# Three row groups of a depthwise convolution on ScalarE and GpSimd, and a new order at the end of each image pair

## The reference

```
g = groupnorm(x)                                   # 32 groups: two channels share mean and variance
t2 = conv(g, w2, 1x3)
t3 = einsum('nakhw,nbhw->nakb', g shifted by 2k-6, g) / 56  # 7 correlations of channels, 64x64
x1 = x + conv5x5(g, w8, depthwise, dilation 2)
       - (correlation weights (t3*p6w*p9w) applied to t2 shifted by 7 rows - conv1x5(t2, w7, depthwise))
t  = tokens of x1 (3136 per image)
a  = layernorm(t); q, k = elu(a Wq)+1, elu(a Wk)+1 (16 heads of 64); v = a Wv
t  = t + linear attention with cosine and sine weights of q, k, v, projected by dense_w
b  = layernorm(t); p = softmax over tokens of (b gate_w + gate_b)   # 32 experts
top = the 8 largest p of each expert; pooled = sum of p * b over them
out = t + (per-expert two-layer MLP of pooled) scattered back with weight p
```

## Time and profile before

| | |
|---|---|
| median of three runs | 4075.51 us |
| profiled execution | 4079.0 us |
| its span | 4077.2 us |
| mean granted clock of TensorE | 0.94 of full |
| TensorE matmul busy | 3586.0 us, 88% |
| VectorE busy | 2994.3 us, 73% |
| ScalarE busy | 1687.9 us, 41% |
| GpSimd busy | 1248.6 us, 31% |

### The profile page before, as it was taken

The page is one execution under the profiler, slowest core; times in us unless marked ns, Lnnn a source line. Parts: engine busy times, 40 slices in busy tenths (PEclk is TensorE's granted clock), DMA queues, the critical chain, the costliest instruction groups (busy, mean ns, idle before and its releaser), DMA issues.

```text
span 4077.2 us, 52073 instructions
## 1 busy us (share of the span) xinstructions
PE 3586.0 (88%) x17556; PEld 1798.3 (44%) x17556; DVE 2994.3 (73%) x3523; ACT 1687.9 (41%) x1798; POOL 1248.6 (31%) x1327
## 2 busy tenths in 40 slices
PE   4798998989889998989889899899989898899976
PEld 2344444444544444444444445344444444544453
DVE  6878876788677876788767886778767887548823
ACT  0145533455254534445434553445435554343310
POOL 1015620176013740156201760127501572011100
PEclk8899998999999998999989999999989999899967
DMA  1000000000000001000000000000010000100045
GB/s 47 17 1 1 1 17 25 1 1 1 25 17 1 1 1 41 1 1 1 17 25 1 1 1 25 17 1 1 1 41 1 1 1 16 30 1 1 1 116 200
DMA packets 18676, 70.96 MB, mean 17 GB/s; under 512 B 8781, under 2 KB 13421, under 8 KB 13485
## 3 DMA queue, kind: packets, MB, share of 16 engines
q1 hardware_dynamic: 18365, 67.10, 5.3%
HBM read 37.26 MB, written 29.84 MB: 16 GB/s over the span
## 4 chain that ended last, share of the span: by engine, by line
issue 48%; PE 33%; DVE 8%; POOL 7%; ACT 2%; DMA 1%; SPq 1%; POOLq 0%; DVEq 0%; ACTq 0%
PE ps_D L1499 11%; POOL UA L549 4%; PE ps_E L1463 4%; PE ps_C L1488 3%; PE ps_A L1446 3%; PE ps_B L1446 3%; DVE RR L1106 2%; PE ps_E L1474 1%; DVE region L1076 1%; DVE arena L911 1%; PE ps_C L1417 1%; POOL RS L581 1%; PE ps_E L1512 1%; POOL RR L574 1%; DVE region L1085 1%
## 5 line engine op out<-in xcount | busy, mean ns | idle before, releaser
L562 POOL TENSOR_TENSOR arena<-arena,UHL 128x896 f32<-128x896 f32 x350 | 764.6, 2210 | 226.3 <-ACT UHL L695 211.6
L1499 PE MATMUL ps_D<-region,small 128*128 128x448 f32 x1792 | 785.2, 562 | 32.9 <-DVE OS L1112 32.8
L549 POOL TENSOR_TENSOR UA<-region,CS 128x128 f32<-128x128 f32 (+1 forms) x400 | 178.8, 449 | 1837.8 <-DVE region L986 795.3
L1085 DVE TENSOR_TENSOR region<-region,ps_C 128x896 f32<-128x896 f32 x448 | 485.9, 1085 | 247.9 <-PE ps_C L1488 247.9
L1499 PEld LDWEIGHTS ps_D<-region,small 128*128 128x128 f32 x1792 | 321.2, 194 | 346.7 <-issue 284.8
L734 ACT ACTIVATE EQ<-ps_B,NEG 128x896 f32<-128x896 f32 x224 | 225.6, 1007 | 480.4 <-PE ps_B L1446 480.3
L911 DVE SCALAR_TENSOR_TENSOR arena<-arena,W8C 128x896 f32<-128x896 f32 (+1 forms) x418 | 416.8, 1010 | 1.2
L1417 PE MATMUL ps_C<-region,UA 128*128 128x512 f32 (+1 forms) x800 | 382.7, 601 | 2.9 <-ACT region L627 2.9
L734 ACT ACTIVATE EQ<-ps_A,NEG 128x896 f32<-128x896 f32 x224 | 225.6, 1007 | 350.8 <-PE ps_A L1446 350.7
L695 ACT ACTIVATE UHL<-arena,W8C 128x896 f32<-128x896 f32 x350 | 361.2, 1032 | 0.0
L1052 DVE SCALAR_TENSOR_TENSOR region<-region,ps_B 128x1024 f32<-128x1024 f32 (+1 forms) x200 | 243.9, 1219 | 159.8 <-ACT region L713 156.4
(11 more groups left out here) (310 smaller groups left out, 5772.9 us busy)
## 6 DMA issues: line engine op xcount, KB each, us to landing
arena<-x SPq DMA_DIRECT2D x8, 1568.0 KB, 6.6
t_keep<-Y SPq DMA_DIRECT2D x7, 1568.0 KB, 6.8
w_keep<-region SPq DMA_DIRECT2D x7, 784.0 KB, 5.7
CST<-t_keep SPq DMA_DIRECT2D x2, 1568.0 KB, 10.0
small<-t_keep SPq DMA_DIRECT2D x2, 1568.0 KB, 12.8
plane<-w_keep SPq DMA_DIRECT2D x4, 784.0 KB, 15.9
UHL<-t_keep SPq DMA_DIRECT2D x2, 1568.0 KB, 12.3
out<-CST SPq DMA_DIRECT2D x2, 1568.0 KB, 11.7
```

The source lines that it names most:

```text
L562: pool.tensor_tensor(out=X[:, cut], in0=X[:, cut], in1=PRODUCT[m % 3], op=ALU.add).then_inc(pool_taps.sem, 1)
L1085: dve.tensor_tensor(out=q, in0=q, op=ALU.mult, in1=here.area(key)[:, :].rearrange("p (c n) -> p c n", c=2)[:, :, 0:PIX])\
L1499: ins = pe.matmul(here.area(key)[:, 0:PIX], MW[i][:, c, :], Q[s % 3][:, c, :], start=c == 0, stop=c == NCHUNK - 1)
```

## The change

- GpSimd and ScalarE take three of the four row groups (75 pieces) instead of two (50). The first 30 of them are done beside K tiles 20 to 49, one per tile, the other 45 in Q slots from slot 3. VectorE keeps the narrow group, 25 pieces, one per K tile from tile 19.
- The square roots of ScalarE and the reciprocals of VectorE in the layer and group norms become a power of -0.5 on GpSimd (`deviations`, `group_norm`), in GpSimd's queue behind the UA product of a tile or the sum of a slot. The scaling of the second layer norm comes one slot later.
- `correlations` and its copies (`columns`) go ahead of the tokens' second transposes and the logits. In `back`, TensorE does two convolutions, two token transposes with the third convolution between them, then weights and pooled tokens, the fourth convolution and the split. VectorE does the maximum, the residuals of groups 0 and 1 around the shares, both layer norms, and the residuals of groups 2 and 3 last. The low part of group 1 goes to K tile 0.
- Pooled tokens are computed with the 64 weight columns in alternating halves of the array, copied, and turned with `BOTH` (both halves' identities), which adds up the halves.
- Tile numbers of norms and splits shift, and PSUM areas are named instead of handed round.

The diff, cut to its core:

```diff
--- before
+++ after
-POOL_UNITS = 2
+POOL_UNITS = 3
 POOL_PIECES = 25 * POOL_UNITS
...
-SUM_TILES = [None, None, 0, 4]
...
-SCALE_TILES = [None, None, 9, 10]
-SPLIT_TILES = [None, None, 11, 12]
-UTS_TILES = [None, 2, 13, 15]
+SUM_TILES = [None, None, 1, 5]
+STD_TILES = [None, None, 6, 10]
+SCALE_TILES = [None, None, 8, 12]
...
 FIRST_TAPS = TAPS[:25 - DIAGONALS] + TAPS[25:]
 FIRST_PIECES = len(FIRST_TAPS) * NG
-STATS_TILE, MEAN_TILE, CENTRE_TILE, VAR_TILE, NORM_TILE = 3, 12, 13, 15, 16
+STATS_TILE, MEAN_TILE, CENTRE_TILE, VAR_TILE, SPREAD_TILE, NORM_TILE = 3, 13, 13, 15, 16, 18
 K_PIECES, FRONT_PIECES, Q_PIECES, DRAIN_PIECES = 1, PIECES, (1, 0, 0, 1), 1
-PRODUCT_SLOT, POOL_LAG = 3, 4
+PRODUCT_TILE, PRODUCT_SLOT, POOL_LAG = 20, 3, 4
+TILE_PRODUCTS = KTILES - PRODUCT_TILE
 SLOTS = 4 * STEPS
 DEN_LAG, SUM_LAG, RECIP_LAG, RB_LAG, OUT_LAG, PARTS_LAG, FOLD_LAG = 4, 5, 6, 8, 9, 13, 18
...
-            uses = [(("ucol", g), misc()) for g in range(len(COLGROUPS))]
-            uses += [("t3", "D")]
-            uses += [(("wt", g), misc()) for g in range(2)] if routing else []
-            uses += [("t3t", misc())] + ([("pool", "E")] if routing else [])
-            for g in range(NG):
-                uses += [(("conv", g), misc())]
-                uses += [(("yt", g - 1), misc())] if g in (1, 2) else []
-                uses += [(("uts", i, 0), misc()) for i in range(2)] if g == 2 else []
-            return uses
+            uses = [("t3t", "C"), (("conv", 0), "A"), (("conv", 1), "B"), (("yt", 0), "C"), (("conv", 2), "A"),
+                    (("yt", 1), "B")]
+            uses += [(("wt", 0), "C"), (("wt", 1), "B"), ("pool", "E")] if routing else []
+            uses += [(("conv", 3), "C")] + ([("pool_turned", "E")] if routing else [])
...
+            def deviations(sums, std, pair, g, turn):
+
+                pool.wait_ge(*sums.at(pair, g + 1))
+                passed(pool)
+                pool.tensor_scalar(ST[:, g % 2, 2, :], ST[:, g % 2, 1, :], 1.0 / C, LN_EPS, ALU.mult, ALU.add)\
+                    .then_inc(variance.sem, 1)
+                pool.wait_ge(*turn)
+                pool.tensor_tensor(out=ST[:, g % 2, 3, :], in0=ST[:, g % 2, 2, :], op=ALU.pow,
+                                   in1=NEGH[:, 0:1].broadcast_to([P, 2 * GROUP])).then_inc(std.sem, 1)
+
+            def group_norm(here):
+
+                pool.wait_ge(*here.emptied("gvar"))
+                pool.tensor_tensor(out=MV[:, 7:8], in0=MV[:, 6:7], in1=NEGH[:, 0:1], op=ALU.pow)\
+                    .then_inc(gn_scale.sem, 1)
+
             def pair_of_images(here):
                 pair = here.pair
+
...
+                        deviations(ln1_sums, ln1_std, pair, STD_TILES.index(k), variance.at(pair, STD_TILES.index(k) - 1))
+                    if here.span == "loop" and k == SPREAD_TILE:
+                        group_norm(here)
+                    if here.span == "loop" and k >= PRODUCT_TILE:
+                        tap_sum(k - PRODUCT_TILE)
...
+                for g in range(2) if here.span == "loop" else ():
+                    deviations(ln1_sums, ln1_std, pair + 1, g, variance.at(pair, 3 + NG + g))
+
+            group_norm(Here("setup"))
+            for g in range(2):
+                deviations(ln1_sums, ln1_std, 0, g, variance.first(g + 1))
             with pool.Fori(0, PAIRS - 1) as pair:
                 pair_of_images(Here("loop", pair))
             pair_of_images(Here("last", PAIRS - 1))
-            pool.wait_ge(*Here("last").emptied("pool"))
+            pool.wait_ge(*Here("last").emptied("pool_turned"))
             pool.memset(OD, 0.0).then_inc(od_zeroed.sem, 1)
...
-                        for g in (2, 3):
-                            deviations(ln1_sums, ln1_std, pair, g)
-                    if k in SPLIT_TILES:
+                    if k in SPLIT_TILES[2:]:
                         high_part(pair, SPLIT_TILES.index(k))
                     if k in UTS_TILES:
                         split_tokens(here, UTS_TILES.index(k))
-                    if k == VAR_TILE and here.span == "loop":
-                        group_norm(here)
+                    if here.span == "loop" and k >= PRODUCT_TILE:
+                        tap_product(here, pair + 1, k - PRODUCT_TILE)
                     if k == TILES + 2:
...
+                    if here.span == "loop" and PRODUCT_SLOT <= j < PRODUCT_SLOT + POOL_PIECES - TILE_PRODUCTS:
+                        tap_product(here, pair + 1, TILE_PRODUCTS + j - PRODUCT_SLOT)
                     if j in LN2_SLOTS:
                         tokens(here, 2, LN2_SLOTS[j])
-                    if j - 5 in LN2_SLOTS:
-                        deviations(ln2_sums, ln2_std, pair, LN2_SLOTS[j - 5])
                     if here.span == "loop" and j in FRONT_SLOTS:
...
-            def group_norm_apply(here):
-                dve.wait_ge(*here.emptied("gvar"))
-                link(dve.reciprocal(MV[:, 7:8], MV[:, 6:7]))
+            def group_norm_spread(here):
+                dve.wait_ge(*here.filled("gvar"))
+                dve.tensor_scalar(MV[:, 6:7], here.area("gvar")[:, 0:1], GN_EPS, None, ALU.add)\
+                    .then_inc(*here.empty("gvar"))
+
+            def group_norm_apply(pair):
+                dve.wait_ge(*gn_scale.at(pair, 1))
                 dve.tensor_scalar(g_window(4, 0, H), X.rearrange("p (h w) -> p h w", w=W),
...
@@ -1011,35 +1038,45 @@
                 link(dve.reciprocal(MX[:, 10:11], MX[:, 9:10]))
                 dve.tensor_scalar(EW, EW, MX[:, 10:11], None, ALU.mult).then_inc(w_ready.sem, 1)
+            def pool_sums(here):
+
+                dve.wait_ge(*here.filled("pool"))
+                dve.tensor_copy(OS[:, 1, 0:P], here.area("pool")[:, 0:P]).then_inc(*here.empty("pool"))
+
             def pooled(here):
-                dve.wait_ge(*here.filled("pool"))
+                dve.wait_ge(*here.filled("pool_turned"))
                 for i in range(2):
                     ins = dve.tensor_copy(
                         PT[0:C, :, bass.ds(2 * here.pair + i, 1)].rearrange("p e a -> p (e a)"),
-                        here.area("pool")[i * C:(i + 1) * C, i * EXPERTS:(i + 1) * EXPERTS])
-                ins.then_inc(*here.empty("pool"))
+                        here.area("pool_turned")[0:C, i * EXPERTS:(i + 1) * EXPERTS])
+                ins.then_inc(*here.empty("pool_turned"))
...
+                    depthwise(here, pair, FIRST_PIECES)
+                else:
+                    depthwise(here, pair, PIECES)
+                    taps(here)
+                    dve.wait_ge(*t_stored.at(before, 1))
+                    routing(here)
+                conv_residual(here, pair, 0)
                 if before is not None:
-                    routing(here)
-                    depthwise(here, pair, 7)
                     shares(here)
+                conv_residual(here, pair, 1)
+                norm_sums(here, 1, ln1_sums, 0)
+                norm_sums(here, 1, ln1_sums, 1)
+                norm1_scale(pair, 0)
                 if before is not None:
-                    depthwise(here, pair, PIECES)
-                else:
-                    depthwise(here, pair, 51)
-                taps(here)
-                if before is None:
-                    depthwise(here, pair, PIECES)
+                    pool_sums(here)
+                low_part(pair, 0)
+                norm1_scale(pair, 1)
                 if before is not None:
-                    dve.wait_ge(*t_stored.at(before, 1))
                     pooled(here)
-                for g in range(NG):
-                    conv_residual(here, pair, g)
-                    if g in (1, 2):
-                        norm_sums(here, 1, ln1_sums, g - 1)
-                        norm1_scale(pair, g - 1)
-                        low_part(pair, g - 1)
+                conv_residual(here, pair, 2)
+                conv_residual(here, pair, 3)
             def k_features(here, k):
...
                         group_norm(pair + 1, k - STATS_TILE)
                     if conv and k == CENTRE_TILE:
                         group_norm_variance(here)
+                    if conv and k == SPREAD_TILE:
+                        group_norm_spread(here)
                     if conv and k == NORM_TILE:
-                        group_norm_apply(here)
+                        group_norm_apply(pair + 1)
                     if conv and k > NORM_TILE:
-                        depthwise(here, pair + 1, K_PIECES)
+                        depthwise(here, pair + 1, K_PIECES, DVE_PIECES)
...
@@ -1161,8 +1200,8 @@
                     for part in range(4):
                         if j - 1 - part in LN2_SLOTS:
                             norm_part(here, 2, ln2_sums, LN2_SLOTS[j - 1 - part], part)
-                    if j - 6 in LN2_SLOTS:
-                        norm_scale(2, ln2_std, pair, LN2_SLOTS[j - 6]).then_inc(un2_ready.sem, 1)
+                    if j - 7 in LN2_SLOTS:
```

(47 more changed lines are left out.)

98 lines of the change are left out of this document (54 added, 44 removed).

## The result

The changed kernel takes 3845.6 us (median of 4 runs, 3844.4 to 3850.3) against 4074.7 us: a ratio of 0.944, 95% interval 0.942 to 0.946. A second measurement on another chip gave 0.9427 (0.9414 to 0.9441). The forecast was 3936 us: the sign and the places were right, the gain was 229 us instead of 139.

The account below looks back on a forecast made before the run. Turns of 478.0 us dominate, with a serial end where VectorE becomes the chain. Terms -12 - 5.5 + 8 - 10 = -19.5 us per turn, times 7, and -3 for the last pair give 3936 us; range 3868 to 4015.

Parts of the forecast that it names:

- shared access: K tiles 20 to 43: VectorE and GpSimd exclude each other, 3.0 us a tile; +8 us per turn, bounds 0 and +30.
- Q steps: Q steps without pieces on VectorE get shorter: sum -10 us per turn, bounds -3 and -14.
- early K tiles: Tiles 0 to 19: two waits and the square roots' table loads go; -5.5 us per turn, bounds -2 and -6.
- pooled tokens: End of turn: column halves take 3.5 us instead of 5.93, all under VectorE's chain, so 0.
- End of turn: Reordered end: next K tile starts at 3035.5 instead of 3047.7; gain 12 us, 8 with more waits, 15 with none.
- first layer norm's pair: Q steps: this step pair becomes like the second one, 39.4 to 33.6 us, -5.8.
- steps 3 to 6: Q steps: four steps of 14.6 us on average become 13.5 without VectorE's pieces, -4.3 us.
- Last pair: After the seven turns: the last pair loses some table loads and cold pooling, about -3 us.
- Rival 4: Nothing lost in the K tiles and no waits at the end: -34.5 us per turn, 3831 us; chance 0.05.
- Rivals 1 and 2: K tiles 20 to 43: VectorE and GpSimd lock step, 4090 us, chance 0.07; Q steps gain nothing, 4006 us, 0.14.
- Rival 3: GpSimd's power is dear: at 6 us each all gain goes, at 8 us 4200 us; chance 0.06.
- the cover: Powers on GpSimd, taken as 1 us each, are hidden by other work at every place: 0.

Follow-up runs that it names:

- e3: Changed kernel with VectorE's 25 narrow pieces moved from K tiles 19 to 43 into Q slots, two per step; ratio 0.959 to the kernel before.
- e11: Changed kernel with all tiles of layer norm, split and mean where the kernel before has them, powers still on GpSimd; ratio 0.952 to the kernel before.
- e12: e11 with square roots of one column back on ScalarE as well; ratio 0.954 to the kernel before.
- e7: Changed kernel plus an unused one-column square root on ScalarE at each power, bringing the table loads back; 3854.5 us.
- e4: Changed kernel with 16 of VectorE's narrow pieces in every second K tile and 9 in the first five Q steps; ratio 0.939 to the kernel before.
- e5: Changed kernel with 16 of VectorE's narrow pieces in every second K tile and 9 in Q steps 2 to 6; 3829.7 us.
- e9: e5 with convolution 2's residual ahead of the pooled copy and the second layer norm's scaling; ratio 0.938 to the kernel before.
- e13: e5 with the pooled copy first, then convolution 2's residual, then the second layer norm's scaling; 3817.9 us against 3829.7 for e5.
- e2: Kernel before with only the pieces' part: three row groups on ScalarE and GpSimd, 30 of 75 pieces beside K tiles; ratio 0.982.

## Why the prediction was off

The mechanisms stood in the right places, and the terms of the sum were mis-sized, all to the same side. The steps that failed: the price of the shared access (+8 us for +3.5), the sum of the Q steps (-10 for -15 to -16), in which the first two steps stood at nothing, and, smaller, the early K tiles and the pooled tokens, which stood at 0. Forecast per turn against measured, in the last turn and as the mean of six:

- **End of turn, -12: measured -11.8, mean -13.4.** Chain, waits (1.8 us for 2.0) and the pooled tokens (3.2 us for 3.5) came as worked out, and the first K tile waits for the residual, as forecast, and for the transposes' copy as well. What failed is the 0 for the pooled tokens. In the kernel before they stand in TensorE's chain ahead of the first convolution, and in three of seven turns they take 9.5 us instead of 5.93, with an end longer by 4.8 us; I had read one turn without it. Now they lie under VectorE's chain at 3.2 and at 4.9 us alike (e3). No run has the new order without the halves, so what the halves alone are worth is open.
- **Early K tiles, -5.5 with -6 as the bound: measured -7.6, mean -6.8.** The tiles' shifts make 4.9 us of the mean (e11). I had summed the two stalls and their half clock and taken the rest for token transposes, which stay; TensorE now has 0.4 us of waits there, so three smaller ones went too: 0.7 us with the tiles (it is back in e11), 0.8 and 0.4 us with the square roots (waits like them are back in e12). The roots are worth about 1 us with the old tiles and 0.7 with the new (e12, e7). Ten of them and the loads back cost 1.3 us in a turn.
- **Shared access, +8: measured +3.5, mean +3.4.** The mechanism is shown (e3: gone with the pieces), the price was 2.79 us a tile instead of 3.0. I added two small gaps that are not there, and 0.47 us of hold where the rows have 0.38 (UA's 0.78 less 0.40): 24 x 0.21 = 5.0 us. The other 1.5 us I put down to the buffers, as in the forecast; no run shows it by itself. "0.78 + 2.08" overlap by 0.07. VectorE's piece waits for the end of GpSimd's sum and UA for the end of the piece; the K feature runs beside the sum. The Trainium skill (SBUF — State Buffer, SBUF: two separate sides) calls this an exclusive lock held for the whole instruction; the trace agrees, with a piece of 1.73 us beside a sum and 0.68 alone.
- **Q steps, -10 with -14 as the bound: measured -16.0, mean -14.9.** The steps that I priced came out: the first layer norm's pair 33.6 us as forecast, steps 3 to 6 -2.8 for -4.3. Not priced were the first two steps: 9.3 and 11.9 us instead of 11.4 and 14.0. I take VectorE for the chain there, as the reciprocal, the split and the scaling have no work ahead of them, and e4 bears it out: with pieces back in these steps they take 3.0 us more. I had looked for what the pieces cost only where I had a pair of equal steps with and without them. Before, TensorE then worked at half clock in step 2, after 2.21 us of waiting: 0.58 us for a Q projection's matmul, 0.35 in the changed kernel. Another 3 us came in the second layer norm's pair and behind the last step. e3 shows that the pieces on VectorE do it: with them back in the Q steps, and GpSimd's work as in the changed kernel, Q is 247.1 us.
- **Last pair, -3: measured -8.8.** Pooled tokens take 5.5 us instead of 11.1 in this colder stretch, of which 4.9 are left behind the turning; the final adds give 3.7 and the K tiles 2.5, and the Q steps take 2.3 more.

Rival 4 (nothing lost in the K tiles, no waits at the end, -34.5 us per turn, 0.05) was nearest in time, but for other reasons, and that is luck: 3.5 us are lost in the K tiles and 1.8 us of waits remain; the Q steps gave 0.9 to 2 us more than its bound, and the slow pooled tokens are in no term of it. Rivals 1 and 2 did not happen. Rival 3's price came out at 2.58 us, above the bound of 2.1 which I took from a sum of 896 elements, and the cover held but for 0.5 us; doubled, it costs 7 us per turn.

## What to carry to other kernels

Price a relieved engine in every stage, and first where the pipeline fills: there each microsecond of it is on the chain, and two pieces cost 1.4 to 1.6 us in the first steps (e4), 0.1 to 0.3 in steps 2 to 4, and 1.2 again in step 5 (e5). Read more than one turn: the one that I read lacked the slow pooled tokens that three of seven have. Where two engines exclude each other, add up who holds the access and for how long; if the sum is just over the period, give every second period to one of them (e4, e5). And when taking away a wait changes nothing (e9), look for a second one that ends at nearly the same time: moving both was worth 0.3% (e13).

## What was not expected of the hardware

A power over 14 elements per partition takes 2.58 us on GpSimd, longer than its sum of 896 elements (2.08), and over 1 element 0.55 us. 50 matmuls of pooled tokens took 5.93 or 9.5 us and, with 128 moving and 64 weight columns, 3.2 or 4.9 us. The 9.55 us of e2 stand in a stretch with a granted clock of 0.65, behind one of 1.00 in which TensorE had been busy for 91%. In the kernel before the same instructions at the same place, behind nearly the same work, ran at a clock of 0.60 in three of seven turns and at 1.00 in the others; what decides it, no run here shows.
